# The first expert layer of a recurrent two-layer kernel: routed in 15 tiles in place of eight dense experts

## The reference

```python
# layer 0, experts: x (b, t, 128), W1 (8, 128, 256), W2 (8, 256, 128)
raw_gate = softmax(x @ gate)                      # over 8 experts
topk_scores, topk_idx = top_k(raw_gate, 2)
gate_topk = mask * raw_gate / max(sum(mask * raw_gate), 1e-12)
h = relu(einsum('btd,edh->beth', x, W1) + b1)
expert_out = einsum('beth,ehd->betd', h, W2) + b2
out = einsum('bte,betd->btd', gate_topk, expert_out)
```

## Time and profile before

| | us |
|---|---|
| runs | 975.25 and 983.37, median 979.31 |
| the profiled execution | 977.57 |
| its span, first to last instruction | 975.8 |

### The profile page before, as it was taken

The page is one execution under the profiler, slowest core; times in us unless marked ns, Lnnn a source line. Parts: engine busy times, 40 slices in busy tenths (PEclk is TensorE's granted clock), DMA queues, the critical chain, the costliest instruction groups (busy, mean ns, idle before and its releaser), DMA issues.

```text
span 975.8 us, 15806 instructions
## 1 busy us (share of the span) xinstructions
PE 854.6 (88%) x4624; PEld 583.0 (60%) x4624; DVE 777.3 (80%) x1479; ACT 632.0 (65%) x1379; POOL 592.7 (61%) x556
## 2 busy tenths in 40 slices
PE   5987898999799978999799979999799967785995
PEld 2773475775467746775567746775567735552662
DVE  3234537899988998799888998799888998877995
ACT  3524735868577775878477766878487765665661
POOL 0010202758856595858866694858766696869675
PEclk9987799999999998999899998999899997877999
DMA  7200103223322432224212332224213332333451
GB/s 265 88 1 13 33 12 98 85 76 123 99 71 75 109 120 85 84 87 132 95 55 87 107 120 75 84 88 133 93 57 106 95 109 98 117 99 95 134 146 52
DMA packets 79429, 90.28 MB, mean 93 GB/s; under 512 B 8450, under 2 KB 49906, under 8 KB 78834
## 3 DMA queue, kind: packets, MB, share of 16 engines
q1 hardware_dynamic: 77298, 85.07, 27.9%
q0 software_dynamic: 2048, 4.20, 1.5%
HBM read 52.96 MB, written 13.04 MB: 68 GB/s over the span
## 4 chain that ended last, share of the span: by engine, by line
PE 53%; POOL 17%; DVE 15%; issue 10%; ACT 4%; SPq 1%; DMA 0%; DVEq 0%; POOLq 0%
PE work L825 9%; PE work L831 7%; POOL st L1474 7%; PE work L856 7%; DVE st L1304 6%; PE work L866 5%; PE yacc L890 5%; POOL y L1481 4%; PE work L754 3%; PE work L775 3%; POOL fe L1461 3%; POOL du L1435 2%; PE work L745 2%; PE work L798 2%; ACT prob L946 1%
## 5 line engine op out<-in xcount | busy, mean ns | idle before, releaser
L1474 POOL TENSOR_TENSOR st<-st,Cs 128x512 f32<-128x512 f32 x249 | 315.9, 1281 | 184.4 <-DVE st L1304 182.2
L946 ACT ACTIVATE dA<-delta,Aneg 128x512 f32<-128x512 f32 x256 | 176.0, 722 | 9.6 <-DVE st L1304 9.1
L1304 DVE TENSOR_TENSOR_SCAN st<-dA,dbu 128x512 f32<-128x512 f32 x128 | 154.8, 1210 | 13.4 <-ACT dA L946 9.2
L890 PE MATMUL yacc<-st,w_ident 128*128 128x512 f32 x256 | 141.3, 637 | 27.2 <-POOL st L1474 27.2
L1304 DVE TENSOR_TENSOR_SCAN st<-dA,b_row 128x512 f32<-128x512 f32 x123 | 148.7, 1209 | 2.9 <-DVE acc L1194 1.5
L831 PEld LDWEIGHTS work<-w_w2a,hid 128*128 128x128 f32 x1024 | 121.5, 192 | 27.6 <-issue 13.0
L825 PE MATMUL work<-xnT,w_w1a 128*128 128x512 f32 x256 | 130.4, 600 | 5.9 <-ACT ys L946 3.8
L1481 POOL TENSOR_TENSOR y<-y,st 128x512 f32<-128x512 f32 x105 | 133.4, 1271 | 2.9
L946 ACT ACTIVATE hsT<-work,hs 128x128 f32<-128x128 f32 x352 | 100.6, 373 | 49.5 <-PE work L856 49.5
L831 PE MATMUL work<-w_w2a,hid 128*128 128x128 f32 x1024 | 124.9, 276 | 7.6 <-DVE delta L1278 7.6
L856 PE MATMUL work<-xsT,hs 128*128 128x128 f32 x704 | 106.6, 303 | 19.1 <-ACT xsT L946 17.9
(11 more groups left out here) (190 smaller groups left out, 1308.3 us busy)
## 6 DMA issues: line engine op xcount, KB each, us to landing
Cs<-c_dram SPq DMA_DIRECT2D x128, 256.0 KB, 3.6
hs<-w_w1f SPq DMA_DIRECT2D x88, 258.0 KB, 2.4
xs_in<-xs_dram SPq DMA_DIRECT2D x16, 256.0 KB, 2.8
ys_dram<-ys SPq DMA_DIRECT2D x16, 256.0 KB, 3.9
w_w1f<-in_w1f_dram SPq DMA_DIRECT2D x1, 2064.0 KB, 8.1
x_in<-in_x_dram SPq DMA_DIRECT2D x8, 256.0 KB, 3.3
w_w2f<-in_w2f_dram SPq DMA_DIRECT2D x1, 2048.0 KB, 12.4
kept_dram<-x_tok SPq DMA_DIRECT2D x8, 256.0 KB, 4.5
```

The source lines that it names most:

```text
L890: mm(yacc[:], ident[:], state(s), start=False, stop=(n == NS - 1)).then_inc(sig["y_sum0"], 1)
L946: return nc.scalar.activation(out, in_, func, **k)
L1304: V.tensor_tensor_scan(state(s), dA[:, s % DECAYS], (dbu0, rows_bank(n, b))[h][:], 0.0, ALU.mult, ALU.add).then_inc(sig["scan"], 1)
L1474: G.tensor_tensor(state(s), state(s), Cs[:, b.of(NS, n) % C_BUFS], ALU.mult).then_inc(sig["P"], 1)
```

## The change

The first experts are routed. For each batch:

- the two choices of a token are kept apart (oh12), and ranks are computed as in layer 1 (PE step "ra", DVE step "ra"): each of 1024 token slots gets a place in a list that is sorted by expert and padded to tiles of 128, at most ST0 = 15 tiles;
- POOL scatters the normalised tokens to DRAM with eight indirect DMAs ("pa"); SP loads them back, four tiles at a time ("la"); PE transposes them ("ta");
- SP fetches W1, W2 and b1 of each tile's expert from DRAM, 263 KB for a tile, into five buffers ("wa"); PE computes "ha" (two tiles at a time) and "ya"; ACT copies and applies relu; SP stores the results ("sa");
- POOL gathers them with eight indirect DMAs ("ga") into fab, which shares its memory with prob; DVE adds gate times result for the two choices ("ca", eight instructions); "silu" works in the bank of b2.

Taken away: the steps "h" and "m", hid, acc, and W1 and W2 in SBUF. In the prologue the stores that blank the scatter area come earlier, and the load of layer 1's expert weights is a step of the order. The whole table ROWS is written anew; below are only the rows that the text speaks of.

```diff
--- before.py
+++ after.py
@@ ROWS (cut) @@
-    ("H", "rk", 0, 0.63158, 7, 0, 2, 1),
-    ("F", "get", 0, 0.80172, 5, 2, 1, None),
-    ("A", "silu", 0, 0.96823, 1, 2, 4, None),
+    ("S", "p", 21, 0.69394, -3, -2, -4, None),
+    ("H", "rk", 0, 0.62847, -1, 1, -2, 1),
+    ("F", "get", 0, 0.80241, -4, 1, 5, None),
+    ("A", "silu", 0, 0.92414, 0, 2, 2, None),
+    ("S", "p", 28, 0.91954, -1, -2, -1, None),
+    ("S", "e", 13, 0.93045, 8, 7, -1, None),
+    ("S", "p", 29, 0.92588, 3, -3, 2, None),
+    ("H", "du", 0, 0.98380, -3, -2, -1, None),
+    ("S", "e", 14, 1.00177, 8, 7, 0, None),
+    ("A", "ra", 0, 0.12860, 4, -1, 8, 3),
+    ("A", "pa", 0, 0.08798, -2, -4, 0, None),
+    ("A", "pa", 7, 0.21329, -4, -4, 0, None),
+    ("A", "ya", 14, 0.81817, 0, 6, 3, 3),
+    ("A", "sa", 3, 0.89176, 7, 6, 7, None),
+    ("A", "ga", 0, 0.93815, 2, 0, -2, None),
+    ("A", "ga", 7, 0.99950, 2, 3, -2, None),
+    ("A", "ca", 0, 0.90288, 4, 2, 5, None),
...
+                elif g == "A" and name == "wa":
+                    if k == 0:
+                        sp.wait_ge(sig["pos0"], b.of(1, 1))
+                    since(sp, sig["y0_in"], b.of(ST0, k - W_BUFS + 1))
+                    e = sp.value_load(texp0[0:1, par, k:k + 1], min_val=0, max_val=E - 1)
+                    sp.dma_start(hs0[:, k % W_BUFS], ins["w0"][0][bass.ds(e, 1)].rearrange("e p k -> (e p) k")
+                                 ).then_inc(w0_ld[k % W_BUFS], 16)
+                elif g == "A" and name == "la":
...
+                        sp.wait_ge(sig["put0"], b.of(16 * 2 * NT, 16 * 2 * NT))
...
-                elif name == "h":
-                    last = mm(w[:], W["w1a"][:, i * 128:(i + 1) * 128], xnT[:], start=True, stop=True)
-                elif name == "m":
...
+                elif name == "ha":
+                    for t in range(2 * i, min(2 * i + 2, ST0)):
+                        pe.wait_ge(w0_ld[t % W_BUFS], b.of(16 * ST0 // W_BUFS, 16 * (t // W_BUFS + 1)))
+                        for c in range(KC):
+                            last = mm(w[:, k:k + 128], hs0[:, t % W_BUFS, c * 128:(c + 1) * 128],
+                                      xsT0[:, t // 4 % 2, t % 4 * 128:(t % 4 + 1) * 128], start=True, stop=True)
+                elif name == "ya":
+                    for c in range(KC):
+                        last = mm(w[:, i % 4 * 128:(i % 4 + 1) * 128], hsT0[:, i // 2 % 2, k:k + 128],
+                                  hs0[:, i % W_BUFS, H0 + c * 128:H0 + (c + 1) * 128], start=(c == 0), stop=(c == KC - 1))
...
+                elif name == "ca":
+                    dve.wait_ge(sig["got0"], b.of(16 * 2 * NT, 16 * 2 * NT))
+                    filled(dve, g, ("b2", 0), b)
+                    for k in range(2):
+                        for t in range(NT):
+                            last = V.scalar_tensor_tensor(r[:, t], fab[:, k, t], gab[:, par, t, k:k + 1], r[:, t], ALU.mult, ALU.add)
...
+                elif name == "pa":
+                    if i == 0:
+                        pool.wait_ge(sig["pos0"], b.of(1, 1))
+                    G.indirect_dma_start(xs0_dram.rearrange("i p d -> (i p) d"),
+                                         bass.IndirectOffsetOnAxis(pos0[:, par, i // 2, i % 2:i % 2 + 1], 0),
+                                         xn_tok[:, i // 2], None).then_inc(sig["put0"], 16)
+                elif name == "ga":
+                    if i == 0:
+                        for k in range(2):
+                            pool.wait_ge(ys0_out[k], b.of(16 * 2, 16 * 2))
+                        filled(pool, g, ("p", NT - 1), b)
+                    G.indirect_dma_start(fab[:, i % 2, i // 2], None, ys0_dram.rearrange("i p d -> (i p) d"),
+                                         bass.IndirectOffsetOnAxis(pos0[:, par, i // 2, i % 2:i % 2 + 1], 0)
+                                         ).then_inc(sig["got0"], 16)
```

More of the change, by code:

```diff
@@ L54, in group_tiles, with first_tiles @@
     return range(4 * k, min(4 * k + 4, ST))
+def first_tiles(k):
+    return range(4 * k, min(4 * k + 4, ST0))
 ROWS = [
[262 rows of a table removed]
[307 rows of a table added]
 ]
@@ L384 @@
 TAKEN_AT = {("A", ("o", 0)): ("o", NT - 1)}
+TAKEN_AT.update({("A", ("ya", 4 * k)): ("ya", first_tiles(k)[-1]) for k in range(NG0)})
 READY = {}
@@ L389 @@
 for _g, _s, _b in ORDER:
-    if (_g, _s) in BANK:
+    if (_g, _s) in BANK and _s[0] != "ya":
         READY[_g, _s, _b] = 1 + sum(1 for g, s, b in READY if g == _g)
@@ L441, in build @@
         for name, (_, shape) in ins.items():
-            if name != "x" and name not in W:
+            if name not in ("x", "w0") and name not in W:
                 W[name] = sb("w_" + name, [128, shape[1]] if name == "dtpT" else shape)
@@ L486, in build @@
         oh1 = sb("oh1", [128, NT, E])
-        oh2 = sb("oh2", [128, NT, E])
+        oh12 = sb("oh12", [128, NT, 2, E])
+        ohb0 = sb("ohb0", [128, NT, E], BF16)
+        slot = sb("slot", [128, NT, 2, E])
+        gab = sb("gab", [128, 2, NT, 2])
+        posf0 = sb("posf0", [128, NT, 2])
+        pos0 = sb("pos0", [128, 2, NT, 2], U32)
+        upto0 = sb("upto0", [1, ST0, E])
+        texf0 = sb("texf0", [1, ST0])
+        texp0 = sb("texp0", [1, 2, ST0], I32)
+        hs0 = sb("hs0", [128, W_BUFS, 2 * H0 + KC])
+        hsT0 = sb("hsT0", [128, 2, 2 * H0])
+        xs_in0 = sb("xs_in0", [128, 4, D])
+        xsT0 = sb("xsT0", [128, 2, T])
+        ys0 = sb("ys0", [128, 8, D])
         gates = sb("gates", [128, NT, E])
-        hid = sb("hid", [128, 4, T])
-        acc = sb("acc", [128, NT, D])
         stats1 = sb("stats1", [128, NT, 6])
@@ L553, in build @@
         ys_out = (sig["ys_out0"], sig["ys_out1"])
+        ys0_out = (sig["ys0_out0"], sig["ys0_out1"])
+        w0_ld = tuple(sig["w0_ld%d" % k] for k in range(W_BUFS))
         w_ld = (sig["w_ld0"], sig["w_ld1"])
@@ L683, in do @@
                                  ).then_inc(sig["xr"], 16)
+                elif g == "P" and name == "sp":
+                    load("ffn1")
                 elif g == "C" and name == "out":
@@ L686, in do, with load @@
                     sp.dma_start(out[b.n].rearrange("(i p) d -> p i d", p=128), ot[:]).then_inc(sig["out"], 16)
+            def load(part):
+                for name in LOADS[part]:
+                    sp.dma_start(W[name][96:96 + RANK] if name == "dtpT" else W[name][:], ins[name][0]).then_inc(loads[part], 16)
             load_x(Batch(0))
-            for part, names in LOADS.items():
-                if part == "mamba":
-                    load_x(Batch(1))
-                for name in names:
-                    sp.dma_start(W[name][96:96 + RANK] if name == "dtpT" else W[name][:], ins[name][0]).then_inc(loads[part], 16)
-            sp.wait_ge(prep_dve, 1)
+            load("small")
+            load("ffn0")
+            sp.wait_ge(sig["blank"], 1)
+            for k in range(NG0):
+                n = len(first_tiles(k))
+                sp.dma_start(xs0_dram[4 * k:4 * k + n].rearrange("i p d -> p i d"), fe[:, 0:n]).then_inc(sig["xs0_zero"], 16)
+            load_x(Batch(1))
+            load("mamba")
             for k in range(NG):
@@ L811, in expert_step @@
                 name, i = step
-                if name not in ("b2", "h", "m"):
+                if name not in ("b2", "ta", "ha", "ya"):
                     return None
-                w = bank(g, step, b)
+                w = None if name == "ya" else bank(g, step, b)
                 if name == "b2":
@@ L952, in a_step @@
                 w = bank(g, step, b) if (g, step) in BANK else None
-                if name == "h":
+                if name == "ta":
                     filled(act, g, step, b)
-                    if i >= 4:
-                        filled(act, g, ("m", i // PER - 2), b)
-                    go(hid[:, i % 4], w[:], ACT.Relu, bias=W["b1a"][:, i:i + 1]).then_inc(fr, 1)
-                elif name == "b2":
-                    filled(act, g, step, b)
-                    since(act, sig["acc"], b.of(E + 1))
-                    go(acc[:], tiles(w[:]), ACT.Copy).then_inc(fr, 1)
+                    if i >= 2:
+                        filled(act, g, ("ha", 2 * i - 3), b)
+                    elif not b.is_(0):
+                        filled(act, g, ("ha", (5, 7)[i]), b + -1)
+                    n = len(first_tiles(i)) * 128
+                    go(xsT0[:, i % 2, 0:n], w[:, 0:n], ACT.Copy).then_inc(fr, 1)
+                elif name == "ha":
+                    filled(act, g, step, b)
+                    since(act, sig["y0_in"], b.of(ST0, 2 * i - 2 if i >= 2 else i - 1))
+                    for t in range(2 * i, min(2 * i + 2, ST0)):
+                        for c in range(KC):
+                            k = (t % 2 * KC + c) * 128
+                            last = go(hsT0[:, i % 2, k:k + 128], w[:, k:k + 128], ACT.Relu,
+                                      bias=hs0[:, t % W_BUFS, 2 * H0 + c:2 * H0 + c + 1])
+                    last.then_inc(fr, 1)
```

(39 more changed lines are left out.)

122 lines of the change are left out of this document (72 added, 50 removed), and 574 rows, old and new, of tables (OWN, ROWS, sig).

## The result

The changed kernel takes 1063.84 us (1063.56 to 1064.11, 2 runs) against 979.31: a ratio of 1.087, 95% interval 1.0812 to 1.0929. It is slower by 84.5 us. The prediction said 1025 us, range 960 to 1070, slower with a chance of 0.64. Its profiled execution has a span of 1062.3 us, 86.5 more than before.

What follows compares the result with a forecast made beforehand. The prediction took PE to set about 70 of 109 us a period, DVE and POOL the remaining 39. Span 975.8 + 18 (prologue) + 29 (periods) = 1023 us, plus 1.8 gives 1025; range 960 to 1070.

Steps and rivals of the forecast that it cites:

- The sum per period: Legs over DVE and POOL in one period add to 116.8 us, taken as 114, bounds 110 and 118.
- e14: POOL's wide instruction ending its 41 us unbroken run in a period; scan 1 of the next batch needs it.
- PE is on no leg of it: In a period, PE's 87 us of work stay hidden behind the queues of DVE and POOL.
- PE sets about 70 of 109 us: Kernel before, one period: chain of waits put about 70 us on PE, the remaining 39 on DVE and POOL.
- sums decide: Rival: DVE and POOL overlap, the period is POOL's 99 us of work, total 936 us; chance 0.16.
- DVE's waits: In a period, DVE idles about 6 us before "ca" for gathers and some 6 for e1 and e2.
- e1: POOL's instruction after the scatters that DVE's scan 7 waits for; with e2, some 6 us of waiting.
- e2: POOL's instruction after the scatters that DVE's scan 9 waits for; with e1, some 6 us of waiting.
- The clock: Rival: PE's clock falls to 0.8, tiles' last store comes late, period 121 us, total 1067 us; chance 0.14.
- Prologue: Before batch 0's x_tok: serial routing of 58 us replaces dense experts, +18 us (8 to 28); batch 1 unchanged at 90.
- the hidden fetches: 15 weight fetches of 263 KB a batch are hidden by five buffers and 100 us for 15 tiles.
- the chain as told: Main case: the chain over DVE and POOL sets the period, total 1000 to 1050 us; chance 0.50.

Runs made afterwards that it cites:

- the kernel with all cuts: Changed kernel with one of eight gathers and scatters, half the tiles' products, ranks reused and no fetches from batch 2, 64 prologue products moved: 991.38 us.
- all three cuts: Changed kernel with one gather and one scatter of eight per batch and one K chunk of two in the tiles' products: 1006.18 us.
- the relieved kernel before: Kernel before the change with most of PE's products for the dense experts left out, everything else kept: 949.43 us.

## Why the prediction came out as it did

- **The sum per period: right in size.** 114 told, 115.75 measured. The prediction added 5 us a period, from 109 to 114; before is 108.4 on this count, and 7.4 were added. The legs, from the end of scan 21 at 499.1 us to that at 615.1: 5.0 us measured (5 told) to put 0, 40.7 (41) to the end of e14, 19.4 (18.5) to the first scatter at 564.2, 20.0 (20) to the end of scan 9, 30.9 (32.3) to scan 21, together 116.0 (116.8). In the next period, of 118.4 us, the third leg is 21.9: DVE waits 3.3 us longer for PE's products of the ranks.
- **"PE is on no leg of it": wrong, and this is the step that failed in its mechanism.** There is a second chain over PE, ACT and DVE of the same length. The chain of waits of the kernel after has 41 of 116 us on PE and 23 on POOL, where "POOL more than 60 us a period, PE hardly" was told; with the scatters out PE has 70. So the price of POOL's DMAs isn't what was argued: 7 of 8 gathers out gives 1.6 us a period, not 8.8. The prediction got the period right from one of several chains that were all near 116.
- **What PE's relief is worth.** The reading "PE sets about 70 of 109 us" came from the earlier trace rows, a chain of last waits. In the kernel before, 20 us less of products shorten the period by 1.4 only. With its lists as they stand, the period of before was held by something else as much as by PE, and PE's relief alone was worth next to nothing; the rival "sums decide" (936 us) falls with it, as even the kernel with all cuts stands at 109.5 a period. The Trainium skill (Perfetto Trace Analysis, Identifying the Most-Contended Engine) was cited for occupancy; the same section says that for PE the busy share of products is no good measure and that its useful operations as a share of the peak, and the share of weight loads, should stand in its place. By the share of weight loads, PE was at 69.6 of 108.9 us, 64%, and DVE at 88% was the fullest. The experiment agrees with this rule and not with the reading of it in the prediction.
- **DVE's waits.** Told: 6 us before "ca" for the gathers. Measured: none there; 7.2 us before scan 29 for PE's b_row, whose queue was late behind tiles and projections. The place was right within ten us, the cause wrong. For e1 and e2 DVE waits 3.9 us in all, 6 told.
- **The clock.** This rival's total, 1067, is closer than the forecast's, but not its mechanism. It wanted a clock of 0.8 from "ta" 0 to ya14, 48 us of PE's work that become 58, and a late last store. The granted clock in that stretch was 0.97, PE was busy 49.8 us in it, and the first gather waited for nothing; the 0.87 of the whole period comes from the stretches around it. And the run without half of the tiles' products, with 8.7 us less of PE's busy time, gained nothing in the steady periods. Its sign to look for, PE on the chain between "ta" 0 and ya14, did appear: the sign did not tell this rival from a chain over PE at full clock. What the lower clock outside that stretch adds to the chain over PE isn't shown.
- **Prologue: the mis-sized term, +42.9 for +18 (8 to 28).** Batch 0 came 7.9 us later than told (89.1 for 81). From the first scatter to x_tok the legs are 11.5 (told 12.3) until the rows have landed, 3.1 (2.8) for the load, 1.8 (0.5) to the first product, **30.0 (20)** for the 15 tiles, 3.9 (4.4) to the first gather, 11.3 (11.7) until the last has landed. The tiles are the error. The prediction counted 1.1 us of PE and 0.2 of waiting for each. The stretch of the tiles:

```profile
39.09:69.04 29.95, 25.17 (x165) 21.35 (x165) 2.32 (x7) 15.80 (x45) 0.00 (x0) 0.89 0.63 168
```

PE is busy 25.2 of the 30.0 us: the tiles' products are 19.8 by their groups (16.5 told), and some 8 us of other products stand between them, the attention's of the same batch above all (the groups overlap a little). These others had no price. PE idles 4.8 us, nearly all of it for ACT's relus and copies (3 told). With half of the products the stretch still takes 26.8 us, but that doesn't speak against PE's part: its granted clock is 0.76 there in place of 0.89, and its busy time falls by 4.5 us only. What the tiles would take without the other products between them isn't shown. Batch 1 was told at the same 90 us and took 106.8: 13.1 of the 17 are the 64 products. The prediction saw them in the list ("the first dl and beta products") and gave them no price. The other 4 weren't traced.
- **End: 0 told, -0.6 measured. ACT at no cost and the hidden fetches: right**, by the runs above for the fetches, by 79.8 against 78.4 us of busy time for ACT.
- **The sum of errors.** Six periods were 15 us longer than told and the prologue 25, together the 39 between 1025 and 1063.8. The measured time lies outside the 1000 to 1050 that the chain as told was given; what held it in the range was the bound at the clock's rival, whose mechanism did not occur. That is luck of a nearby number. (The step is also summed a little short: (114 - 109) * 6 is 30, not 29.)

What stays open is what holds the period near 111 with all three cuts, and how the 8.5 us between the relieved kernel before (107.0) and the kernel after (115.5 a period, the mean of the three runs of it with no cut that shortened a period) divide: the cuts on DMAs, products, ranks and fetches bring back 6.0 of them, the tiles' chain, the gates' slots and the new places, which no run removed, may hold the rest. That the kernel's two chains share a piece, and that they are just two, is argued and not shown.

## What to carry to other kernels

In a kernel whose engines' lists were placed against each other, the chain of waits can name one of several chains of equal length; before pricing a change by it, look for the second one through every other engine, for a cut on one may then return a fifth or less (here 1.6 us for 8.8). A relief of one engine is worth what the others leave. Price every item that the new order puts into a serial prologue, the once-only preparations too, and where short tiles share an engine's list with other work, price that work too: in the serial stretch it was 8 of 30 us.

## What the chip showed that was not expected

- The same 64 one-column products took 13.8 us in the kernel after, at a granted clock of 0.50 over that stretch (the level of 1.2 GHz), and 9.85 us where they follow the attention's products of batch 0 directly (0.71). Ahead of the slow ones PE was busy 19.8 of the 38 us from 89 to 127; ahead of the fast ones, 12.3 of the 13 us from 60 to 73, at a granted clock of 1.00. The stretch in the kernel after (columns as in the earlier trace rows):

```profile
127.20:140.90 13.70, 13.70 (x66) 13.68 (x65) 0.71 (x5) 2.50 (x4) 3.83 (x4) 0.50 0.19 56
```

And in the kernel with the 64 products moved:

```profile
73.20:83.00 9.80, 9.80 (x66) 9.76 (x64) 0.00 (x0) 0.00 (x0) 6.78 (x8) 0.71 0.21 52
```

- The mean clock of a period hides where it is low: 0.87 over a period of the kernel after is 0.97 from 580 to 633 us, where PE is busy 93%, and 0.63 from 633 to 658, where it is busy 56%.
- PE gives back part of a relief: with 20 us of products taken from a period of the kernel before, its busy time fell by 13.3, with the clock at 0.92 for 0.97.
- Fifteen fetches of 257 KB from DRAM a batch, each landing 3.1 us after issue, cost nothing: the period is 116 us with them and without (DMA share 0.51 and 0.40).
